# A two-layer graph attention kernel: first loads in another order, first projection spread over ten slots, one unit's copies on VectorE

## The chip, the cores and the metric

The kernel runs on 1 core of one Trainium2 chip. The metric is device time in microseconds (us) from the start to the end of an execution. The engines are TensorE (PE; its weight loads are shown as PEld), VectorE (DVE), ScalarE (ACT), GpSimd (POOL) and SyncE (SP). SP issues every transfer of this kernel, and 16 DMA engines carry it out.

## What is computed

x is 128 graphs of 128 nodes with 384 numbers each, adj is 128 matrices of 128x128. Each of two layers adds a 12-headed attention over a normalised x; the two layers differ in where adj enters and in the projection at the end.

```
h = max(layernorm(x), 0)
q, k, v = h @ W0q + b0q, h @ W0k + b0k, h @ W0v + b0v            # 12 heads of 32
a = softmax(where(adj > 0, q k^T / sqrt(32) + beta * adj, -9e15))
x = x + a v

h = max(layernorm(x), 0)
q, k, v = h @ W1q.T, h @ W1k.T, h @ W1v.T + b1v
a = q k^T / sqrt(384) + adj        # a row of zeros alone gives zeros
x = x + (softmax(a) v) @ W1o.T + b1o
```

## The kernel before

Four graphs (512 tokens) make a group, a group in one layer makes a unit: 64 units. The program is a row of phases of 12 slots each, and in a phase several units are in different stages at once: one is normalised (`norm`), one projected (`project`), one attended (`attend`), and the last chunks of the one before are finished (`tail`). A slot is a chunk of attention: 4 heads of one graph, so 3 slots are a graph. Each engine runs its own in-order program, and semaphores tie them together. Where in a slot a step stands is set by hand, by constants such as `SPLIT_AT = (2, 0)` (slots later, place in the slot), and by tables.

*Normalising.* VectorE makes the statistics of a graph (L813 to L825), ScalarE centres it (L717). For the first two units ScalarE also makes the fp16 high half (L726) and VectorE the low half (L835); SP then turns both into h by a DMA transpose (L518), one a graph. GpSimd raises the variance to -0.5 (L568).

*Weights.* Seven weights are loaded (L457, `load_weight`) and split into w_hi (ScalarE, L658) and w_lo (VectorE, L766), in slots given by LOAD_SLOTS, HIGH_SLOTS and LOW_SLOTS. The first three are staged in the buffers that later hold the stacks.

*Projecting.* A unit has ten jobs of nine matmuls (L999, `job_bank`): six for q and k, four for v. PROJ tables say how many of them stand at three places of each slot. ScalarE makes part_hi of a q or k job (L679, L683), VectorE part_lo (L865, L870); VectorE takes v (L879). SP copies each part_hi twice and each part_lo once into "stack" (L483, L487): 18 copies of 128 KB a unit. The first unit's first copy waits for the third w_lo, since a stack lies over its staging. The scores (L1012) of the third chunk need the last of these copies, and the first matmul of a unit's projection needs all four of its transposes.

*Attention.* In slot s PE makes the scores of chunk s+2, VectorE turns those of chunk s+1 into neg and neg_max (L787), ScalarE takes the exponentials of chunk s (L667), PE transposes the probabilities of chunk s-1 into pt_bank (L1022), and they are copied to probs_t (L692, ScalarE). Three chunks on, PE multiplies them with v (L1035, `o_bank`). In layer 1 five small VectorE steps, reciprocal to inv_wide (L844 to L857), PE's transpose (L1058) and ScalarE's copy inv_t (L699) prepare the scaling; o_norm (L893, VectorE), o_hi (L706, ScalarE), o_lo (L644, GpSimd), the output projection (L1068 to L1072) and result_rows (L901, VectorE) follow. GpSimd adds up neg (L599, L605).

*First phases.* Phase 0 normalises unit 0 and converts three weights. Phase 1 projects unit 0 by PROJ_FIRST, normalises unit 1 (x_second, which lies in probs_t) and makes the first two chunks' scores. Phase 2 attends unit 0 and projects unit 1. The last unit has a phase in which its v is projected by PROJ_LAST_V beside its own attention.

Of the kernel before, what the change touches and what calls it, by code (L numbers as in the profile page):

```python
# [15 lines left out]
KC = DIM // P  # L16
# [30 lines left out]
PROJ_FIRST = ((0, 0, 0),) * 4 + ((4, 4, 3),) * 6 + ((4, 4, 4),) * 2  # L47
PROJ_LAST_QK = ((0, 4, 1), (1, 4, 0), (0, 4, 1), (4, 0, 1), (0, 4, 1), (5, 0, 1), (4, 1, 1), (2, 2, 1), (4, 4, 2),
                (2, 0, 0), (0, 0, 0), (0, 0, 0))
PROJ_LAST_V = ((0, 0, 5), (0, 0, 4), (0, 0, 0)) * GROUP  # L50
# [31 lines left out]
NORM_SLOTS_FIRST = (0, 1, 2, 3)  # L82
SHARED_UNITS = 2
LOW_ROWS_AT = (3, 0)

LOAD_SLOTS = ({}, {}, {0: 3, 3: 4, 6: 5, 9: 6}, {})
HIGH_SLOTS = ({2: 0, 3: 1, 5: 2}, {}, {3: 3, 6: 4, 9: 5}, {0: 6})
LOW_SLOTS = ({4: 0, 6: 1, 8: 2}, {}, {4: 3, 7: 4, 10: 5}, {1: 6})
# [41 lines left out]
class Phase:  # L130
# [9 lines left out]

    def counts(self):
        return self.table or PROJ[self.attend.layer]
# [21 lines left out]
def before():  # L164
# [3 lines left out]
        Phase(project=u(0), norm=u(1), look=u(0), bias=0, weights=1, table=PROJ_FIRST, norm_slots=NORM_SLOTS_FIRST),  # L168
# [81 lines left out]
def layer1_unit(group, off):  # L250

    if not isinstance(group, int):
        return group * 2 + (2 * off + 2)
    return next(n for n in range(UNITS) if layer_and_group(n) == (1, group + off))

# [14 lines left out]
def build(nc, x, adj, w0q, b0q, w0k, b0k, w0v, b0v, beta, w1q, w1k, w1v, b1v, w1o, b1o, out):  # L270
    weights = (w0q, w0k, w0v, w1q, w1k, w1v, w1o)
    w_scale = (QK0_SCALE, QK0_SCALE, W_SCALE, W_SCALE, W_SCALE, W_SCALE, W_SCALE)
    with ExitStack() as ctx:
# [176 lines left out]
        def _(sp):  # L450
# [3 lines left out]
            load_first(0)  # L454
            load_first(1)
            def load_weight(m):
                sp.dma_start(staging(m), weights[m].rearrange("(c p) n -> p c n", p=P)).then_inc(weight_in[m], 16)  # L457

            load_weight(0)
            load_first(2)  # L460
            load_first(3)
# [9 lines left out]
            load_weight(2)  # L471
# [18 lines left out]
            def phase(p):  # L490
                for s in range(SLOTS):
# [38 lines left out]
                    if s == 10 and p.norm is not None and p.norm.layer == 0:  # L530
                        g = p.norm.group
                        if isinstance(g, int) and g < 2:

                            if g == 1:
                                sp.wait_ge(centred_ready, GROUP)
                                sp.dma_start(x_norm[:, :, :], x_groups[2]).then_inc(x_norm_in, 16)
                        elif not isinstance(g, int) or g < GROUPS - 1:
                            sp.wait_ge(centred_ready, p.norm.n * GROUP + GROUP)
                            sp.dma_start(x_norm[:, :, :], x_groups[g + 1]).then_inc(x_norm_in, 16)
                    if p.weights == 0 and s == 5:  # L540
                        sp.dma_start(x_second, x_groups[1]).then_inc(x_second_in, 16)
# [3 lines left out]
            phase(before()[0])  # L545
            sp.dma_start(adj0[:, :, :], adj_groups[0]).then_inc(adj0_in, 16)
            phase(before()[1])
            sp.dma_start(x_res[:, :, :], x_groups[0]).then_inc(x_res_in, 16)
# [106 lines left out]
        def _(act):  # L655
# [73 lines left out]
            def phase(p):  # L729
                for s in range(SLOTS):  # L730
                    for place in range(4):
# [3 lines left out]
                        if place == 2 and u is not None:  # L735
                            copy_turned(u, c)
# [22 lines left out]
        def _(dve):  # L759
# [9 lines left out]
            def biased_scores(u, c):  # L769
# [21 lines left out]
                last.then_inc(neg_ready, 1)  # L791

# [119 lines left out]
            def phase(p):  # L912
                bias_slot = SLOTS - 1 if p.attend is not None else 7
                for s in range(SLOTS + 1):
                    for place in range(3):
# [6 lines left out]
                        if place == 1 and u is not None:  # L922
                            biased_scores(u, c)
# [210 lines left out]
```

## Time and profile before

| | us |
|---|---|
| median of 3 runs | 2221.32 |
| lowest, highest | 2221.24, 2221.51 |
| profiled execution | 2218.76 |
| its span, first to last instruction | 2216.9 |

| engine | busy, share of the span |
|---|---|
| PE | 97% |
| ACT | 92% |
| DVE | 82% |
| POOL | 68% |
| PEld | 64% |

All rows below come from the one profiled execution, with times from the start of its span. A share is an average over all stages; the first 50 us and the last 40 us look different from it, and are read in the timeline and in windows. Operations of one engine overlap a little, so the distance from one start to the next is shorter than the length that is shown.

### The profile page before, as it was taken

The page shows a single profiled execution, that of the slowest core. Times are in us where ns is not written, and L with a number is a line of the kernel's source. Part 1 is how long each engine was busy: PE and PEld are TensorE (multiplying, and loading weights), DVE is VectorE, ACT ScalarE, POOL GpSimd, SP SyncE. Part 2 cuts the span into 40 slices and gives each one's busy share as a digit, 9 for nine tenths or more (in the row PEclk, how much of TensorE's full clock was granted, in tenths as well). Part 3 has the DMA queues.
Part 4 walks back from the last instruction along what each step waited for, and adds up shares of the span by engine and source line. Part 5 has one row for each costly group of instructions (what it writes and reads, how often), then busy time and mean ns, then how long its engine had stood idle before and what let it go on. Part 6 is the DMA issues. An engine that isn't in the chain of part 4 may idle for free.

```text
span 2216.9 us, 75650 instructions
## 1 busy us (share of the span) xinstructions
PE 2158.5 (97%) x19968; PEld 1422.1 (64%) x19968; DVE 1821.3 (82%) x10202; ACT 2049.2 (92%) x7824; POOL 1511.6 (68%) x2407
## 2 busy tenths in 40 slices
PE   5999999999999999999999999999999999999997
PEld 2566666666666666666666666666666666666665
DVE  5888888888888888888888888888888888888787
ACT  4999999999999999999999999999999999999987
POOL 1567766767667767667676677676676766776665
PEclk9999999999999999999999999999999999999999
DMA  9886776678678778675795686787767866766752
GB/s 191 168 134 140 130 138 147 130 131 157 126 137 138 137 143 141 132 143 125 134 159 127 136 139 136 145 136 137 143 130 135 154 130 134 146 132 134 133 103 60
DMA packets 461362, 303.38 MB, mean 137 GB/s; under 512 B 228481, under 2 KB 460929, under 8 KB 460929
## 3 DMA queue, kind: packets, MB, share of 16 engines
q1 hardware_dynamic: 460928, 298.45, 71.2%
q8 instruction: 169, 2.77, 0.6%
q14 instruction: 265, 2.16, 0.4%
HBM read 71.83 MB, written 25.17 MB: 44 GB/s over the span
## 4 chain that ended last, share of the span: by engine, by line
PE 84%; DVE 7%; ACT 4%; issue 3%; DMA 1%; SPq 0%; DVEq 0%; POOL 0%; ACTq 0%
PE job_bank L999 46%; PE pt_bank L1022 13%; PE o_bank L1035 8%; PE score_bank L1012 7%; ACT probs L667 3%; PE inv_bank L1058 3%; PE post_bank L1068 2%; PE post_bank L1069 2%; PE post_bank L1072 2%; PE post_bank L1050 2%; DVE neg L787 2%; DVE part_lo L865 1%; DVE inv_wide L857 1%; DMA x_norm<-in_x 1%; DVE off_zero L848 1%
## 5 line engine op out<-in xcount | busy, mean ns | idle before, releaser
L667 ACT ACTIVATE probs<-neg,neg_max 128x128 f32<-128x128 f32 x3072 | 1189.8, 394 | 47.0 <-DVE neg_max L787 47.0
L999 PE MATMUL job_bank<-h,w_hi 128*128 128x512 f16 x2304 | 725.9, 381 | 27.1 <-DMA h<-o_norm 21.6
L667 ACT ACTIVATION_READ_ACCUMULATOR probs<-neg,neg_max 128x1 f32 x3072 | 596.0, 194 | 0.0
L692 ACT ACTIVATE probs_t<-pt_bank 128x512 f32<-128x512 f32 x768 | 450.1, 586 | 32.0 <-PE pt_bank L1022 29.2
L1022 PE MATMUL pt_bank<-ident,probs 128*128 128x128 f32 x3072 | 464.2, 274 | 11.8 <-ACT probs_t L692 11.4
L999 PE MATMUL job_bank<-h,w_lo 128*128 128x512 f16 x1152 | 438.4, 381 | 0.0
L1022 PEld LDWEIGHTS pt_bank<-ident,probs 128*128 128x128 f32 x3072 | 365.9, 141 | 95.9 <-issue 14.0
L599 POOL TENSOR_TENSOR pair_sum<-neg 128x256 f32<-128x256 f32 x384 | 281.0, 732 | 196.0 <-DVE neg_max L787 180.8
L999 PE MATMUL job_bank<-w_hi,h 128*128 128x384 f16 x1536 | 413.9, 326 | 0.6 <-DVE v L879 0.3
L787 DVE CUSTOM_DVE_ANT_0 neg<-score_bank,bias 128x128 f32<-128x128 f32 x1536 | 354.1, 286 | 23.7 <-issue 22.2
L787 DVE CUSTOM_DVE_ANT_0 neg<-score_bank,adj 128x128 f32<-128x128 f32 x1536 | 353.8, 286 | 13.2 <-issue 10.5
L999 PEld LDWEIGHTS job_bank<-h,w_hi 128*128 128x128 f16 x2304 | 222.0, 98 | 217.4 <-issue 35.8
L1012 PEld LDWEIGHTS score_bank<-stack 96*128 96x128 f16 x3072 | 232.4, 97 | 126.5 <-DVE neg_max L787 6.3
L1012 PE MATMUL score_bank<-stack 96*128 96x128 f16 x3072 | 299.2, 219 | 5.3 <-DMA stack<-part_lo 5.3
L787 DVE DVE_READ_ACCUMULATOR2_ANT neg_max<- 128x1 f32 x3072 | 254.3, 83 | 0.6
L999 PE MATMUL job_bank<-w_lo,h 128*128 128x384 f16 x768 | 250.5, 326 | 0.0
L568 POOL TENSOR_TENSOR rstd<-shift_var,minus_half 128x1 f32<-128x1 f32 x256 | 144.8, 566 | 146.9 <-DVE shift_var L825 145.4
L590 POOL TENSOR_TENSOR h_rows<-h_rows 128x384 f16<-128x384 f32 x248 | 226.7, 914 | 20.7
L618 POOL TENSOR_TENSOR x_mid<-x_res,o_rows 128x384 f32<-128x384 f32 x128 | 127.9, 999 | 140.8 <-DVE o_rows L908 97.1
L1035 PE MATMUL o_bank<-probs_t,v 128*32 128x128 f32 x6144 | 220.8, 277 | 0.0
L870 DVE SCALAR_TENSOR_TENSOR part_lo<-job_bank,part_hi 128x512 f16<-128x512 f32 x192 | 132.5, 690 | 105.4 <-ACT part_hi L683 103.4
L605 POOL TENSOR_TENSOR four_sum<-pair_sum 128x128 f32<-128x128 f32 x384 | 176.6, 460 | 32.1
(75 smaller groups left out, 3507.6 us busy)
## 6 DMA issues: line engine op xcount, KB each, us to landing
stack<-part_hi SPq DMA_DIRECT2D x768, 128.0 KB, 3.5
stack<-part_lo SPq DMA_DIRECT2D x384, 128.0 KB, 3.8
x_res<-in_x SPq DMA_DIRECT2D x32, 768.0 KB, 5.8
out_x<-result_rows SPq DMA_DIRECT2D x128, 192.0 KB, 3.4
x_norm<-in_x SPq DMA_DIRECT2D x30, 768.0 KB, 6.2
adj<-in_adj SPq DMA_DIRECT2D x64, 256.0 KB, 3.8
h<-h_rows SPq DMA_TRANSPOSE x252, 3.9
x_norm<-in_x SPq DMA_DIRECT2D x4, 192.0 KB, 4.0
```

The costliest lines, as they stand in the source:

```text
L568: pool.tensor_tensor(rstd[:, b:b + 1], shift_var[:, b, 1:2], minus_half[:, :], ALU.pow).then_inc(rstd_done, 1)
L590: pool.tensor_tensor(h_rows[b % 2][:, 1, :], h_rows32[:, :], h_rows[b % 2][:, 0, :], ALU.subtract).then_inc(h_rows_ready, 1)
L599: pool.tensor_tensor(pair_sum[:, :, :], neg[c % 2][:, :, 0:NODES // 2], neg[c % 2][:, :, NODES // 2:NODES], ALU.add).then_inc(pair_sum_don ...
L605: pool.tensor_tensor(four_sum[b % 2][:, first:first + HC, :], pair_sum[:, :, 0:NODES // 4], pair_sum[:, :, NODES // 4:NODES // 2], ALU.add ...
L667: last = act.activation(probs[c % 2][:, h, :], neg[c % 2][:, h, :], ACT.Exp, bias=neg_max[:, b, first + h:first + h + 1], scale=-1.0, accu ...
L692: act.activation(probs_t[b % 2][:, first:first + HC, :].rearrange("p h q -> p (h q)"), pt_bank[:, :], ACT.Copy).then_inc(probs_t_ready, 1)
L787: last = dve.tensor_tensor_reduce(out=neg[c % 2][:, h, :], in0=score_bank[c % 2][:, P * h:P * (h + 1)], in1=bias, scale=(-1.0 / SCORE0 if ...
L870: last = dve.scalar_tensor_tensor(part_lo[t][:, c, :], job_bank[j % 2][:, :], scale, part_hi[t][:, c, :], ALU.mult, ALU.subtract)
L999: last = pe.matmul(to, stationary, moving, start=(m == 0), stop=(m == MATMULS - 1))
L1012: last = pe.matmul(score_bank[c % 2][:, P * h:P * (h + 1)], q[0:3 * HEAD, c % KC, h, nodes], k[0:3 * HEAD, c % KC, h, nodes], start=True, ...
L1022: last = pe.transpose(pt_bank[:, P * h:P * (h + 1)], probs[c % 2][:, h, :], ident[:, :])
L1035: last = pe.matmul(o_bank[d:d + HEAD, f:f + P], v32[u.parity][:, b, HEAD * h:HEAD * (h + 1)], probs_t[b % 2][:, h, :], start=True, stop=True)
```

## The change

- The four blocks of the first group's x are loaded ahead of all weights. The third weight is loaded in slot 7 of phase 0, behind the four transposes. The conversions of the three weights move to slots 4 to 9.
- x of the second group, adj of the first, x_norm of the third group and x_res are issued between phase 0 and phase 1. The last two stood in and behind phase 1.
- PROJ_FIRST: 9 matmuls in each of the first ten slots, in place of four empty slots and then 11 or 12. The second unit is normalised in slots 2 to 5 in place of 0 to 3, and its transposes stand correspondingly later.
- PROJ_LAST_V: 3 matmuls in each slot. In that phase (`alone`) the scores stand at place 0 of a slot, not at place 4.
- The last unit's 12 copies of pt_bank are VectorE's, at place 2 of the slot.

```diff
-PROJ_FIRST = ((0, 0, 0),) * 4 + ((4, 4, 3),) * 6 + ((4, 4, 4),) * 2
+PROJ_FIRST = ((3, 3, 3),) * 10 + ((0, 0, 0),) * 2
...
-PROJ_LAST_V = ((0, 0, 5), (0, 0, 4), (0, 0, 0)) * GROUP
+PROJ_LAST_V = ((0, 0, 3),) * SLOTS
...
+NORM_SLOTS_SECOND = (2, 3, 4, 5)
...
-LOAD_SLOTS = ({}, {}, {0: 3, 3: 4, 6: 5, 9: 6}, {})
-HIGH_SLOTS = ({2: 0, 3: 1, 5: 2}, {}, {3: 3, 6: 4, 9: 5}, {0: 6})
-LOW_SLOTS = ({4: 0, 6: 1, 8: 2}, {}, {4: 3, 7: 4, 10: 5}, {1: 6})
+LOAD_SLOTS = ({7: 2}, {}, {0: 3, 3: 4, 6: 5, 9: 6}, {})
+HIGH_SLOTS = ({4: 0, 5: 1, 7: 2}, {}, {3: 3, 6: 4, 9: 5}, {0: 6})
+LOW_SLOTS = ({6: 0, 7: 1, 9: 2}, {}, {4: 3, 7: 4, 10: 5}, {1: 6})
...
+        self.alone = begin > 0
...
+def turned_by_vector(u):
+
+    return isinstance(u.n, int) and u.n == UNITS - 1
...
-            load_first(0)
-            load_first(1)
...
+            for b in range(GROUP):
+                load_first(b)
             load_weight(0)
-            load_first(2)
-            load_first(3)
             load_weight(1)
...
             phase(before()[0])
+            sp.dma_start(x_second, x_groups[1]).then_inc(x_second_in, 16)
             sp.dma_start(adj0[:, :, :], adj_groups[0]).then_inc(adj0_in, 16)
+            sp.wait_ge(centred_ready, GROUP)
+            sp.dma_start(x_norm[:, :, :], x_groups[2]).then_inc(x_norm_in, 16)
+            sp.dma_start(x_res[:, :, :], x_groups[0]).then_inc(x_res_in, 16)
             phase(before()[1])
-            sp.dma_start(x_res[:, :, :], x_groups[0]).then_inc(x_res_in, 16)
...
-                        if place == 2 and u is not None:
+                        if place == 2 and u is not None and not turned_by_vector(u):
                             copy_turned(u, c)
...
+            def copy_turned(u, c):
+                dve.wait_ge(probs_turned, chunk(u, c))
+
+                b, first = c // KC, c % KC * HC
+                if first == 0 and some(u.n * GROUP + b - 1):
+                    dve.wait_ge(pv_done, u.n * GROUP + b - 1)
+                dve.tensor_copy(probs_t[b % 2][:, first:first + HC, :].rearrange("p h q -> p (h q)"),
+                                pt_bank[:, :]).then_inc(probs_t_ready, 1)
...
-                        if place == SCORES_AT and u is not None:
+                        if place == (0 if p.alone else SCORES_AT) and u is not None:
```

SP at the end of phase 0, before: the third weight (its destination is called "stack" there) is issued ahead of the transposes of h, and x of the second group (destination probs_t) ahead of the fourth.

```order
L457 DMA stack<-in_L_gnn_Wv 128x3x384
L518 DMA_TRANSPOSE h<-h_rows 128x6x128 [waits h_rows_ready] x2
L518 DMA_TRANSPOSE h<-o_t 128x6x128 [waits h_rows_ready]
L541 DMA probs_t<-in_x 128x4x384
L518 DMA_TRANSPOSE h<-o_norm 128x6x128 [waits h_rows_ready]
L546 DMA adj<-in_adj 128x4x128
L518 DMA_TRANSPOSE h<-h_rows 128x6x128 [waits h_rows_ready] x2
L518 DMA_TRANSPOSE h<-o_t 128x6x128 [waits h_rows_ready]
L483 DMA stack<-part_hi 32x4x512 [waits part_hi_ready,w_lo_ready]
```

The same place of the changed kernel:

```order
L523 DMA_TRANSPOSE h<-h_rows 128x6x128 [waits h_rows_ready] x2
L523 DMA_TRANSPOSE h<-o_t 128x6x128 [waits h_rows_ready]
L523 DMA_TRANSPOSE h<-o_norm 128x6x128 [waits h_rows_ready]
L463 DMA stack<-in_L_gnn_Wv 128x3x384
L545 DMA probs_t<-in_x 128x4x384
L546 DMA adj<-in_adj 128x4x128
L548 DMA x_norm<-in_x 128x4x384 [waits centred_ready]
L549 DMA x_res<-in_x 128x4x384
L488 DMA stack<-part_hi 32x4x512 [waits part_hi_ready,w_lo_ready]
```

Five loads now stand between the fourth transpose and the first stack copy, and the second unit's transposes moved behind stack copies.

VectorE on the last unit, before: the end of a chunk's score work, then o_norm, v, and the next chunk.

```order
L787 ISA neg,neg_max<-score_bank,adj 128x128
L787 ISA neg_max 128x1
L893 TENSOR_TENSOR o_norm<-o_bank,inv_t 128x384 [waits o_lo_ready,inv_t_ready,pv_done]
L879 SCALAR_TENSOR_TENSOR v<-job_bank,bv_rows 128x384 [waits pv_done,job_done]
L762 MEMSET carrier_v 128x1 [waits pair_sum_done,exp_done,scores_done]
```

The same place, changed:

```order
L789 ISA neg,neg_max<-score_bank,adj 128x128
L789 ISA neg_max 128x1
L801 COPY probs_t<-pt_bank 128x512 [waits probs_turned]
L904 TENSOR_TENSOR o_norm<-o_bank,inv_t 128x384 [waits o_lo_ready,inv_t_ready,pv_done]
L764 MEMSET carrier_v 128x1 [waits pair_sum_done,exp_done,scores_done]
```

A copy stands between a chunk's score work and o_norm, and v has gone one slot later.

PE on the last unit, before: the transpose of inv_wide, v matmuls, and then the scores.

```order
L1058 MATMUL inv_bank<-ident,inv_wide 128x128 [waits inv_t_ready,inv_wide_ready]
L1058 MATMUL inv_bank<-ident,inv_wide 128x128 x2
L999 MATMUL job_bank0<-w_hi5,h1 128x384 x2
L999 MATMUL job_bank0<-w_lo5,h1 128x384
L999 MATMUL job_bank0<-w_hi5,h1 128x384
L1012 MATMUL score_bank1<-stack11,stack01 128x128 [waits neg_ready]
```

Changed, the same scores:

```order
L1026 MATMUL score_bank1<-stack11,stack01 128x128 [waits neg_ready]
L1026 MATMUL score_bank1<-stack11,stack01 128x128 x3
L1082 MATMUL post_bank<-w_hi6,o_hi 128x384 [waits o_hi_ready,result_ready]
L1083 MATMUL post_bank<-w_lo6,o_hi 128x384
L1082 MATMUL post_bank<-w_hi6,o_hi 128x384
L1083 MATMUL post_bank<-w_lo6,o_hi 128x384
```

They now stand ahead of the output projection, the product with v and the transpose of inv_wide in that slot.

## Rows read from the trace of the kernel before

**Rows 1.** The page: an engine's busy time, share of the span, number of instructions.
```profile
PE 2158.5 (97%) x19968; PEld 1422.1 (64%) x19968; DVE 1821.3 (82%) x10202; ACT 2049.2 (92%) x7824; POOL 1511.6 (68%) x2407
```

**Rows 2.** Timeline, 0 to 22 us: start, length, engine, line, operation, [idle before <-released by].
```profile
7.66 0.56 DVE L813 BATCH_NORM_STATS2 stats<-x_norm 128x6 f32<-128x384 f32 x1 [2.50 <-DMA x_norm<-in_x]
...
8.86 4.33 SPq L518 DMA_TRANSPOSE h<-h_rows  x2
...
12.83 0.61 DVE L835 SCALAR_TENSOR_TENSOR o_norm<-inv_wide,rstd,o_norm 128x384 f16<-128x384 f32 x1 [0.56 <-DVE o_t L835]
...
14.98 1.16 ACT L658 ACTIVATE w_hi<-stack 128x1152 f16<-128x1152 f32 x1 [2.19 <-DMA stack<-in_L_gnn_Wv]
...
15.88 1.22 SPq L518 DMA_TRANSPOSE h<-o_norm  x1
...
16.17 1.36 DVE L766 SCALAR_TENSOR_TENSOR w_lo<-stack,w_hi 128x1152 f16<-128x1152 f32 x1 [1.46 <-ACT w_hi L658]
...
21.58 1.01 PE L999 MATMUL job_bank<-h,w_hi 128*128 128x512 f16 x2 [21.58 <-DMA h<-o_norm]
```

**Rows 3.** DMA issues, 0 to 22 and 23 to 27.5 us: KB each, us to landing.
```profile
probs_t<-in_x SPq DMA_DIRECT2D x1, 768.0 KB, 5.5
...
h<-o_t SPq DMA_TRANSPOSE x1, 2.8
```

**Rows 4.** Windows, all engines: us, busy (count) PE PEld DVE ACT POOL, PEclk, DMA, GB/s.
```profile
36.00:47.00 11.00, 7.76 (x50) 4.29 (x48) 5.15 (x24) 3.98 (x17) 0.00 (x0) 1.00 1.17 130
...
48.00:54.00 6.00, 4.75 (x21) 3.19 (x22) 2.70 (x24) 1.53 (x5) 0.73 (x3) 0.50 1.08 354
```

**Rows 5.** Timeline, 40 to 52 us.
```profile
40.53 0.60 SPq L487 DMA_DIRECT2D stack<-part_lo  x1
...
49.25 0.61 PE L1012 MATMUL score_bank<-stack 96*128 96x128 f16 x4 [5.30 <-DMA stack<-part_lo]
...
51.20 0.56 DVE L813 BATCH_NORM_STATS2 stats<-x_norm 128x6 f32<-128x384 f32 x1 [6.46 <-DMA x_norm<-in_x]
...
51.68 0.29 DVE L787 CUSTOM_DVE_ANT_0 neg<-score_bank,bias 128x128 f32<-128x128 f32 x1
```

**Rows 6.** The stack copies of part_hi (L483), 0 to 60 us: issue lengths, and landing.
```profile
L483 SPq DMA_DIRECT2D stack<-part_hi x14: 573/602/700, 28.1 to 56.4; - x14
...
DMA to landing us min/median/max: 2.9/4.3/7.8
```

**Rows 7.** Windows of three graphs of the last unit, columns as in rows 4.
```profile
2177.33:2185.34 8.01, 6.87 (x75) 5.05 (x74) 5.97 (x38) 7.45 (x33) 5.32 (x8) 1.00 0.09 28
...
2185.34:2192.86 7.52, 6.38 (x71) 4.71 (x70) 6.76 (x38) 6.96 (x31) 5.65 (x9) 1.00 0.08 27
...
2192.86:2200.38 7.52, 6.38 (x71) 4.71 (x70) 6.44 (x38) 6.95 (x31) 6.70 (x10) 1.00 0.08 29
```

**Rows 8.** Timeline, 2171 to 2211 us.
```profile
2171.34 0.69 DVE L870 SCALAR_TENSOR_TENSOR part_lo<-job_bank,part_hi 128x512 f16<-128x512 f32 x1 [1.25 <-ACT part_hi L683]
...
2171.95 0.22 DVE L844 RECIPROCAL inv<-total 128x12 f32<-128x12 f32 x1
...
2173.59 0.28 DVE L787 CUSTOM_DVE_ANT_0 neg<-score_bank,adj 128x128 f32<-128x128 f32 x1
...
2182.70 0.29 DVE L787 CUSTOM_DVE_ANT_0 neg<-score_bank,adj 128x128 f32<-128x128 f32 x1 [1.80 <-POOL pair_sum L599]
...
2185.69 0.73 POOL L599 TENSOR_TENSOR pair_sum<-neg 128x256 f32<-128x256 f32 x1
...
2185.89 0.56 DVE L848 TENSOR_SCALAR off_zero<-neg_max 128x12 f32<-128x12 f32 x1
...
2188.32 0.28 DVE L787 CUSTOM_DVE_ANT_0 neg<-score_bank,adj 128x128 f32<-128x128 f32 x1
...
2210.43 0.49 ACT L699 ACTIVATE inv_t<-inv_bank 128x384 f32<-128x384 f32 x1 [2.14 <-PE inv_bank L1058]
```

**Rows 9.** VectorE's copies out of PSUM (L886): min/median/max ns, first and last start.
```profile
L886 DVE COPY o_t<-o_bank x128: 546/557/559, 62.4 to 2113.9; 128x384 f32<-128x384 f32 x128
```

More of the change, by code:

```diff
@@ L167, in before @@
         Phase(norm=u(0), weights=0, norm_slots=NORM_SLOTS_FIRST),
-        Phase(project=u(0), norm=u(1), look=u(0), bias=0, weights=1, table=PROJ_FIRST, norm_slots=NORM_SLOTS_FIRST),
+        Phase(project=u(0), norm=u(1), look=u(0), bias=0, weights=1, table=PROJ_FIRST, norm_slots=NORM_SLOTS_SECOND),
         Phase(attend=u(0), project=u(1), norm=u(2), look=u(1), bias=1, weights=2),
@@ L470, in _ @@
             sp.dma_start(bo_rows[:, :], b1o.partition_broadcast(P)).then_inc(consts_in, 16)
-            load_weight(2)
             def stack(u, j):
@@ L531, in phase @@
                         g = p.norm.group
[L532 to L537, printed above, removed]
+                        if not isinstance(g, int) or 2 <= g < GROUPS - 1:
                             sp.wait_ge(centred_ready, p.norm.n * GROUP + GROUP)
                             sp.dma_start(x_norm[:, :, :], x_groups[g + 1]).then_inc(x_norm_in, 16)
-                    if p.weights == 0 and s == 5:
-                        sp.dma_start(x_second, x_groups[1]).then_inc(x_second_in, 16)
                     if p.weights is not None and s in LOAD_SLOTS[p.weights]:
@@ L923, in phase @@
                             biased_scores(u, c)
+                        u, c = unit_of_chunk(p, s - 1)
+                        if place == 2 and u is not None and turned_by_vector(u):
+                            copy_turned(u, c)
                         u, b = finished(p, s, place, O_T_AT)
```

## The prediction

> **What bounds the kernel now.** The totals come first: PE is busy 97% of a 2216.9 us span [rows 1]. The slices show that its clock and its business are flat from the second slice to the last but one, so the steady part can't be touched by this change, which edits the first 50 us and the last 35 us. What an edit there is worth is the shift it gives to everything behind it. The profiled execution took 2218.76 us, 1.9 more than its span, and 2.6 less than the median of the runs, 2221.32. I make the sum against the profiled one and carry the difference over. The measurement tells about 0.2%, 4.4 us, from no change.
>
> *The start*, read in the timeline. VectorE idles 2.50 us at 7.66 for the third block of x, which was issued behind the first weight; the low half of the fourth block of h ends at 13.44; its DMA transpose is issued at 15.88, behind the 768 KB of the next x, and takes until 21.58, 5.7 us, when PE starts [rows 2]. Then comes the part that is easily missed. The score operands are built by 18 copies of 128 KB ("stack") from 28.1 on [rows 6]. They are issued every 0.65 us, the last at 40.53, but the DMA engines are full from 36 to 47 us at 130 GB/s, which is 1.01 us for a copy [rows 4, 5]. Their time from issue to landing grows from 2.9 us [rows 6] to 8.7, until PE gets the third chunk's operands at 49.25, after 5.30 us of idling, and VectorE, which waits 6.46 us for the next x_norm, gives its third chunk only at 51.68 [rows 5]. Behind that stand ScalarE's exponentials and the whole rest. So the end of the start is set by the DMA engines, not by PE.
>
> *The end*. On the last unit a graph takes 7.52 us; ScalarE is busy 6.96 of them, VectorE 6.76 and 6.44, PE 6.38 [rows 7]. ScalarE is the nearest to a bound, but VectorE follows at once.
>
> **The start, step by step.** All four blocks of x now come ahead of the weights. The 2.50 us wait goes, and the two conversions of 1.36 us stand behind the fourth block [rows 2]; ScalarE's own row of four centre and four high operations keeps a part of that, so I put the last low half at 10.4, not 13.44 (estimate). SP reaches its first transpose when it has issued the constants, at 7.1. Two transposes took 4.33 us to issue, one 1.22 [rows 2]; so the fourth is issued at about 12.8. It lands in 2.8 us when the queue is empty [rows 3], in 5.7 behind the large load [rows 2]; 3.1, near the empty case: PE starts at 15.9 instead of 21.58.
>
> That gain of 5.7 us is not carried on. The third weight is now issued behind the transposes, at 14.1. 768 KB alone took 5.5 us [rows 3], 576 KB some 5.0, so it lands at 19.1. Its two conversions take 1.16 and 1.36 us [rows 2], the bias columns 0.4, and ScalarE's first part_hi waits for these; with 0.7 for itself it ends at 22.8, and the first stack copy goes out then: 5.3 us ahead of 28.1 [rows 6]. PE finishes its first two jobs and waits 1 to 2 us for it. SP waits there as well (stack waits for the third w_lo), and behind it stand only stack copies and the second unit's transposes.
>
> The DMA engines have more in front of them, though: the third weight, x of the second group, adjacency, x_norm and x_res, 3.2 MB, where the last two (1.5 MB) used to come behind the stack copies. At 354 GB/s [rows 4] that is 9.0 us from 16 on: 25. The first stack copy then lands at about 26.3 instead of 31.0. Between 31.0 and 49.25 seventeen further copies and one transpose landed [rows 5, 6]: 17 x 1.01 leaves 1.0 for the transpose. In the change all four transposes of the second unit's h stand behind the fourth copy group or later, the last two behind all copies, and PE's first matmul of the next phase waits for the last: 26.3 + 17.2 + 4.0 = 47.5. It runs two matmuls at the lower clock (0.50 of full speed, 1.2 GHz, is granted there after the idling [rows 4]; PE will have idled from about 39, so again) and the scores, 1.4 us in all: VectorE's third chunk starts at 48.9 instead of 51.68, because its x_norm is long in. **Start: -2.8 us.** If the transposes are issued in 1.22 us each and the loads follow sooner, it is -4.6; if the loads run at the rate of their mixed windows and the first copy lands at 28.5, -0.8.
>
> The Trainium skill, "DMA: Bandwidth & Descriptors", section "Queues, rings and completion order", says that each DMA engine takes a ring's descriptors in order. That speaks against moving two large loads ahead of small urgent copies; by it the 1.5 MB cost the copies their full 4.3 us, as in my sum, and if the engines shared instead, the first copies would land about 2 us sooner.
>
> Norms of the second unit one slot or two later, and PE's even distribution over ten slots, cost nothing: both lie beside the full DMA engines.
>
> **The end, step by step.** Twelve copies of 128x512 go from ScalarE to VectorE. A VectorE operation of the same size out of PSUM lasts 0.69 us and the next starts 0.61 after it [rows 8]: three are 1.83 us for a graph. VectorE's 6.60 (mean of the two windows) become 8.43, more than the 7.52 of a graph now. So VectorE becomes the bound of the last unit. The bounds of its 6.60: the five small steps that make inv_wide run from 2171.95 to 2173.59, 1.64 us; on the last unit they run from 2185.34, where the second window begins, to 2188.32, 2.98 us, and off_zero in them took 0.56 and ended with GpSimd's pair_sum, issued first [rows 8]. GpSimd is busy 5.65 to 6.70 of 7.52 us [rows 7], and in the change its sums still fall beside them; I take 2.6. Without waits a graph would be 7.45, with all of them 8.8. Copies out of PSUM are not stretched: 128 of them took 546 to 559 ns [rows 9].
>
> The Trainium skill, "SBUF — State Buffer", section "SBUF: two separate sides", calls this an exclusive lock of a port pair, held for a whole instruction, that VectorE takes with two SBUF inputs or in a two-port mode. By it the stretch belongs to the small steps alone, as the rows have it, and the period lies in my bounds.
>
> Graph by graph: the first window (8.01 us) has 1.80 us of idle VectorE for scores that PE issued late [rows 7, 8]. Scores at place 0 take that away; but the inverse still waits for PE's transpose behind the output projection, and ScalarE for VectorE's o_norm, which is now behind a copy: 8.6, +0.6. Two full graphs: 2 x 0.91 = +1.8. From the tenth slot's inverse on, ScalarE has no copies left, the last exponentials start 0.5 sooner, and PE's last transposes don't wait for two ScalarE copies in a row: inv_t, at 2210.43 now [rows 8], comes 1.2 us sooner relative to that inverse. **End: +1.2 us** (-1.6 without waits for GpSimd, +3 with all).
>
> **Sum.** 2218.76 - 2.8 + 1.2 = 2217.2 for the profiled execution, 2219.7 for the median.
>
> **Rivals**, each in terms of the median. (a) *VectorE isn't held by GpSimd in the new order*: a period of 7.45, end -1.6, sum -4.4: 2216.9. For it speaks 1.64 us at 2171.95; against it the 2.98 us of the graph at 2185.34. 0.13. (b) *The DMA engines aren't the bound of the start*: the 5.3 us of the first stack copy come through: -4.1, 2217.2. The full window at 130 GB/s speaks against it. 0.10. (c) *The gain of the start is nil*: PE starts early, but the second h's transposes, now last, land at 49 or later: only the +1.2 of the end stays, 2222.5. It needs a first copy at 29; 0.12. (d) *Slower*: VectorE's copies put PE's transposes, which need the bank, into a round trip with it: exponentials, transpose 0.6, copy 0.6, and each small step stretched, so that a graph takes over 9.3 us. Four graphs at +2, less 1.2, less the start: +4, 2225.3. A bank is free only when VectorE has come round to it, which speaks for it; that the copy stands right behind 0.86 us of score work, longer than the transpose needs, against it. 0.05.
>
> **Numbers.** The forecast has 0.60, with its own range 2217.5 to 2221.5. The range down to 2216.0 takes in (a) and (b), up to 2223.0 takes in (c). Faster by over 0.2%: only where a good start and a good end meet, 0.18. Slower by over 0.2%: (d), 0.05. Within: 0.77.
>
> **What would show it.** PE's first matmul at 15.9 and first stack copy issued near 22.8; DMA engines full until 47; PE idle from 39 to 47; VectorE's third chunk at 48.9. On the last unit VectorE busy over 95%, ScalarE idle over 1.5 us a graph, a period of 8.4. I'm wrong if the period is under 7.7 or the third chunk stands before 46.5 or after 51.

## The result, and the profile after

| | before | after |
|---|---|---|
| median of 8 runs, us | 2221.22 | 2214.74 |
| lowest, highest | 2217.97, 2223.24 | 2211.43, 2217.28 |
| profiled execution, its span | 2218.76, 2216.9 | 2216.25, 2214.4 |

The ratio is 0.9972, 95% interval 0.9961 to 0.9983: 6.2 us faster (3.8 to 8.7). The forecast was 2219.7 with a range from 2216.0 on, so the kernel is faster than the whole range, 2216.0 to 2223.0. The profiled execution of before lies 2.5 us under its median, that of the change 1.5 us above; why is read below under *The middle*.

*The start.* Timeline of the changed kernel, 7 to 48 us (start, length, engine, line, operation, [idle before <-released by]); lines have moved: L488, L492 are the stack copies, L523 the transposes of h, L1013 the jobs, L789 the score work.

```profile
16.03 1.01 PE L1013 MATMUL job_bank<-h,w_hi 128*128 128x512 f16 x2 [16.03 <-DMA h<-o_norm]
...
22.31 1.33 SPq L488 DMA_DIRECT2D stack<-part_hi  x2
...
30.23 1.25 SPq L523 DMA_TRANSPOSE h<-h_rows  x1
...
42.89 1.01 PE L1013 MATMUL job_bank<-h,w_hi 128*128 128x512 f16 x2 [4.14 <-DMA h<-o_t]
...
44.38 0.28 DVE L789 CUSTOM_DVE_ANT_0 neg<-score_bank,bias 128x128 f32<-128x128 f32 x1 [3.31 <-issue]
...
47.02 0.06 DVE L764 MEMSET carrier_v<- 128x1 f32 x1 [1.29 <-PE score_bank L1026]
```

PE starts at 16.03 and the first copy is issued at 22.31, both as forecast. But PE gets the last of the four transposed blocks at 42.89, not at 47.5, and the third chunk stands at 44.38, 7.3 us ahead of 51.68 [rows 5]. Why shows in the landing times of the copies of part_hi (L488, up to 40 us) and in the windows (us, busy (count) PE PEld DVE ACT POOL, PEclk, DMA, GB/s). The last window is one of the kernel before, just ahead of that of [rows 4]:

```profile
DMA to landing us min/median/max: 3.4/4.0/4.6
```

```profile
27.00:32.00 5.00, 4.71 (x24) 2.10 (x23) 4.05 (x16) 4.45 (x8) 1.09 (x2) 1.00 1.14 231
34.00:37.00 3.00, 2.49 (x17) 1.30 (x15) 2.20 (x8) 0.00 (x0) 0.00 (x0) 1.00 1.25 134
```

```profile
29.00:36.00 7.00, 7.00 (x33) 3.14 (x33) 4.20 (x8) 2.31 (x4) 0.00 (x0) 1.00 1.04 164
```

The first twelve copies, issued ahead of the first transpose, moved at 231 GB/s in this window, 0.57 us each. From the first landing (22.31 + 4.3 = 26.6) to the twelfth (29.5 + 3.6 = 33.1) it is 0.59 us each, less than the 0.65 us in which SP issues them: the time to landing shrinks and no backlog builds up. The six copies behind them share the queue with transposes, at 134 GB/s, and the landing grows to 5.3 us. Before, two stretches have to be told apart. The first six copies landed from 31.2 to 35.5, 0.86 us each (the window at 164 GB/s holds transposes too). Behind them the fourth transpose was issued, at 32.15, and from then on it is the 130 GB/s of [rows 4]; the last twelve copies landed from 37.5 to 49.2, 1.06 us each.

Part of the 7.3 us goes at once. PE comes out of 4.14 us of idling at half clock, and VectorE waits 1.29 us for the fourth chunk's scores: it stands at 47.05 against 53.06, 6.0 us earlier. Before, PE came back at half clock as well, at 49.25, but it was ahead of VectorE, which waited for x_norm until 51.20 [rows 5]. As the landmark for the start I use from here on the sixth copy o_t<-o_bank: 104.40 before, 98.19 after, **-6.2 us**.

*The middle.* The shift of the copies o_t<-o_bank is still -6.0 us at 994.21 (1000.20 before) and -3.0 at 1041.54 (1044.53 before). In between lies a seam of the program where PE stops for some 3 us. PE's timeline and a window of the changed kernel:

```profile
1026.23 0.61 PE L1013 MATMUL job_bank<-h,w_hi 128*128 128x512 f16 x1 [3.13 <-issue]
```

```profile
1024.00:1036.00 12.00, 9.77 (x68) 6.28 (x69) 6.13 (x40) 6.96 (x28) 2.53 (x5) 0.72 0.05 14
```

PE stood still for 3.13 us (before: 2.67) and then ran until 1032 at half clock, which it didn't in the profiled execution of before, where the granted clock of this window is 1.00. That is scatter of single executions, some 3 us, and not the change. The run end_only below has the start of before, stood still for 2.65 us at the seam, and ran at half clock there too (granted 0.68 from 1030 to 1035). The medians show the whole 6 us, the two profiled executions only 2.5. Similar stretches at half clock stand near 2174 and 2206 us in some of the traces below. For that reason the landmarks, and not the ends of the spans, are compared here.

*The end.* Windows of the three graphs that answer to [rows 7]:

```profile
2174.37:2182.68 8.31, 8.06 (x84) 5.64 (x83) 7.78 (x40) 7.26 (x34) 6.01 (x9) 1.00 0.08 27
2182.68:2190.76 8.08, 6.98 (x71) 4.51 (x70) 7.84 (x39) 5.63 (x27) 5.69 (x9) 1.00 0.07 25
2190.76:2198.49 7.73, 7.04 (x70) 4.53 (x69) 7.49 (x40) 5.63 (x27) 6.71 (x10) 1.00 0.08 29
```

In the two full graphs (the last two lines) VectorE is busy 97% and is the bound, as forecast; ScalarE has 2.1 to 2.5 us to spare. From the second inverse (2174.37) to the last result the unit takes 37.06 us, before 36.60: **+0.46 us**.

### The profile page after: what moved, and what is told of

It is laid out like the page before. It is cut to its first block, busy times and chain, and to the rows that moved or that the text cites. A ratio compares the mean times of both kernels' runs of the same rounds, so it can differ in the third digit from the quotient of the medians.

```text
span 2214.4 us, 75651 instructions
## 1 busy us (share of the span) xinstructions
PE 2163.4 (98%) x19968; PEld 1422.9 (64%) x19968; DVE 1825.4 (82%) x10214; ACT 2043.8 (92%) x7812; POOL 1510.6 (68%) x2407
## 4 chain that ended last, share of the span: by engine, by line
PE 83%; DVE 8%; ACT 4%; issue 3%; SPq 1%; DMA 1%; DVEq 0%; POOL 0%; ACTq 0%; POOLq 0%
PE job_bank L1013 45%; PE pt_bank L1036 13%; PE o_bank L1049 7%; PE score_bank L1026 7%; PE inv_bank L1072 3%; ACT probs L669 3%; PE post_bank L1082 2%; PE post_bank L1086 2%; PE post_bank L1083 2%; PE post_bank L1064 2%; DVE neg L789 2%; DVE part_lo L876 1%; DVE inv_wide L868 1%; DVE live L863 1%; DVE row_sum L857 1%
## 5 line engine op out<-in xcount | busy, mean ns | idle before, releaser
L1013 PE MATMUL job_bank<-h,w_hi 128*128 128x512 f16 x2304 | 726.6, 381 | 26.1 <-DMA h<-o_norm 16.0
L694 ACT ACTIVATE probs_t<-pt_bank 128x512 f32<-128x512 f32 x756 | 443.0, 586 | 31.5 <-PE pt_bank L1036 28.7
L1013 PE MATMUL job_bank<-h,w_lo 128*128 128x512 f16 x1152 | 438.5, 381 | 0.0
L1013 PE MATMUL job_bank<-w_hi,h 128*128 128x384 f16 x1536 | 415.2, 326 | 1.2 <-DVE v L890 0.8
L789 DVE CUSTOM_DVE_ANT_0 neg<-score_bank,bias 128x128 f32<-128x128 f32 x1536 | 354.0, 286 | 29.1 <-issue 27.5
L789 DVE CUSTOM_DVE_ANT_0 neg<-score_bank,adj 128x128 f32<-128x128 f32 x1536 | 353.8, 286 | 10.1 <-issue 9.1
L1013 PEld LDWEIGHTS job_bank<-h,w_hi 128*128 128x128 f16 x2304 | 222.0, 98 | 216.3 <-issue 30.1
L789 DVE DVE_READ_ACCUMULATOR2_ANT neg_max<- 128x1 f32 x3072 | 254.2, 83 | 0.6
L1013 PE MATMUL job_bank<-w_lo,h 128*128 128x384 f16 x768 | 250.5, 326 | 0.0
```

What stands on the lines that cost most here:

```text
L694: act.activation(probs_t[b % 2][:, first:first + HC, :].rearrange("p h q -> p (h q)"), pt_bank[:, :], ACT.Copy).then_inc(probs_t_ready, 1)
L789: last = dve.tensor_tensor_reduce(out=neg[c % 2][:, h, :], in0=score_bank[c % 2][:, P * h:P * (h + 1)], in1=bias, scale=(-1.0 / SCORE0 if ...
L1013: last = pe.matmul(to, stationary, moving, start=(m == 0), stop=(m == MATMULS - 1))
```

## The experiments

"Landmark" is the sixth o_t copy, relative to the 104.40 of before; "unit" is the last unit from its second inverse to its last inv_t (L699 or L701), 33.10 us before and 33.56 after. Both come from one profiled execution of each kernel. Ratios are to the kernel before, with a 95% interval.

| run | third chunk at | landmark | unit | ratio |
|---|---|---|---|---|
| after | 44.38 | -6.2 | 33.56 | 0.9972 (0.9961 to 0.9983) |
| start_only | 45.53 | -6.0 | | 0.9976 (0.9966 to 0.9986) |
| end_only | 51.66 | -0.1 | 33.57 | 1.0004 (0.9995 to 1.0013) |
| loads_behind | 47.81 | -3.7 | 33.56 | 0.9985 (0.9975 to 0.9994) |
| loads_ahead | 51.20 | +0.3 | | 0.9997 (0.9988 to 1.0006) |
| loads_right_ahead | 52.31 | +1.9 | 33.10 | 1.0016 (1.0006 to 1.0026) |
| norm_early | 47.05 | -4.2 | | 0.9978 (0.9968 to 0.9988) |
| proj_packed | 51.07 | -0.1 | 33.55 | 0.9999 (0.9989 to 1.0009) |
| later1_act | 43.83 | -7.5 | 31.83 | 0.9952 (0.9938 to 0.9966) |
| later2_split | 43.37 | -8.4 | 31.75 | 0.9956 (0.9942 to 0.9969) |
| later2_act | 42.52 | -8.6 | 31.81 | 0.9955 (0.9942 to 0.9969) |

Where "unit" is empty, a stretch at half clock lies in it. The third chunk scatters more than the landmark: start_only has the same start as the changed kernel, and 45.53 and 44.38 come together again at -6.0 and -6.2.

**The two halves of the change.** start_only has PROJ_LAST_V, the place of the scores and ScalarE's copies as before; end_only is the kernel before with these three changed.

> The changed kernel with its last unit as before (PROJ_LAST_V, place of the scores, ScalarE's copies): the start of the change alone. The forecast's sum has -2.8 us for it. The trace of the changed kernel has its later start at -6.1 us from 84 us on, so by it: third chunk of VectorE at 44.4, the steady part 6.1 us earlier, and the median 6 us under that of the kernel before (2215.2). If the last unit's edits had brought part of the 6.5 us, the start alone would show under 5 us.

> The kernel before with the last unit of the change (v spread over all slots, scores at place 0, twelve copies on VectorE): the end alone. The forecast has +1.2 us for it; the trace of the changed kernel shows the stretch from the first inverse of the last unit to the last result 0.46 us longer. So: +0.5 us by the trace, +1.2 by the forecast, and periods of 8.3, 8.1 and 7.7 us for the three graphs. If the two parts depend on each other (they are 2100 us apart) it would be another number; I expect none.

Start -6.0 at the landmark, end +0.47 (33.57 against 33.10) and no more than +2.9 us by the interval of end_only. At the landmarks they add up to the change; by the medians they are -5.3 and +0.9 against -6.2, which agrees within the intervals. The gain is the start's alone.

**Which loads stand ahead of the copies.** loads_behind:

```diff
+                        if isinstance(g, int) and g == 1:
+                            sp.wait_ge(centred_ready, GROUP)
+                            sp.dma_start(x_norm[:, :, :], x_groups[2]).then_inc(x_norm_in, 16)
...
-            sp.wait_ge(centred_ready, GROUP)
-            sp.dma_start(x_norm[:, :, :], x_groups[2]).then_inc(x_norm_in, 16)
-            sp.dma_start(x_res[:, :, :], x_groups[0]).then_inc(x_res_in, 16)
             phase(before()[1])
+            sp.dma_start(x_res[:, :, :], x_groups[0]).then_inc(x_res_in, 16)
```

> The changed kernel with x_norm loaded in slot 10 of phase 1 and x_res behind phase 1, as in the kernel before; the stack copies then stand behind 1.7 MB less of loads. Theory A (backlog): copies into bands of 32 partitions are slow, 1.01 us each at 130 GB/s, when the 16 DMA engines reach each of them together, and fast when they come behind a long queue, in which the engines drift apart and work at different copies. Then the copies here run near 130 GB/s from 26 us on, the last transposes land at 45 to 47, and VectorE's third chunk comes at 47 to 50 instead of 44.4: taking 1.5 MB from ahead of them makes them later. Theory B (the rate has nothing to do with the loads; it comes from the order of copies and transposes): the copies run at 180 to 230 GB/s as in the changed kernel, start to land 3 us sooner and are done by 39; the third chunk then waits for x_norm or comes at 42 to 44.

With 1.5 MB less ahead of them the copies are slower: timeline and a window of this run,

```profile
45.23 1.01 PE L1014 MATMUL job_bank<-h,w_hi 128*128 128x512 f16 x2 [6.18 <-DMA h<-o_t]
...
47.32 0.56 DVE L825 BATCH_NORM_STATS2 stats<-x_norm 128x6 f32<-128x384 f32 x1 [6.42 <-DMA x_norm<-in_x]
```

```profile
26.00:34.00 8.00, 7.72 (x39) 3.50 (x38) 6.50 (x24) 7.03 (x12) 1.65 (x3) 1.00 1.16 146
```

PE gets its operands at 45.23 instead of 42.89, and VectorE's x_norm comes later still: it is this wait that sets the third chunk here, at 47.81. The place of the two loads is worth 2.5 us of the 6.2, by both waits together. Theory B falls, since it had 180 to 230 GB/s here. But this run changes two things at once: the loads that are left landed at 22.0, so the queue was empty when the first copy was issued, at 22.63. Which of the two it is, the programs with nothing but copies have to tell.

loads_ahead and loads_right_ahead put the same two loads into the kernel before, once between the phases, once directly ahead of the first stack copy.

> The kernel before with x_norm and x_res issued between phase 0 and phase 1, and nothing else. Theory A (backlog): 1.5 MB stand ahead of the copies, yet these run at 200 GB/s or more once they come (from 32 us on), and the last one lands at 43 to 45 instead of 48: third chunk at 45 to 47 instead of 51.7, the median 4 to 6 us less. Theory B (copies cost 1.01 us each whatever stands ahead): the first copy lands at 32 to 35 and the last at 50 to 52: third chunk at 51 to 53, no gain.

> The kernel before with x_norm and x_res (1.5 MB) issued immediately ahead of the first stack copy, and nothing else; the DMA engines then have a queue of several us when the copies come, which they hadn't in the run with these loads between the phases (there the loads had landed at 27, 2 us before the first copy, and the copies ran at 130 GB/s). Theory A (backlog): the loads end at 33 to 34, the copies behind them run at 200 GB/s or more at first and the last lands at 44 to 47; PE gets the third chunk's operands 2 to 5 us earlier than at 49.25. Theory B (1.01 us a copy, whatever stands ahead): the last copy lands at 51 to 53, the third chunk comes at 52 to 54, the median is 0 to 2 us more than before.

Neither gains, and this took me a step further. In the first the loads had landed by 27.9 us, 1.2 us before the first copy was issued at 29.09, and three transposes stood between: no run of copies behind loads at all. In the second:

```profile
34.00:37.00 3.00, 3.00 (x17) 1.56 (x16) 1.09 (x2) 1.37 (x2) 0.00 (x0) 1.00 1.15 223
39.00:50.00 11.00, 4.17 (x30) 2.23 (x27) 3.97 (x22) 3.29 (x16) 0.00 (x0) 0.88 1.16 132
```

Theory A's fast copies are there, at 223 GB/s, but only six of them: behind these the fourth transpose was issued, at 32.89, and from 39 on it is 132 GB/s for the other twelve. My expectation missed since it took the fast rate to hold to the end. The suspicion: a transpose ends it.

**The other two parts of the start.** norm_early has NORM_SLOTS_SECOND = (0, 1, 2, 3), proj_packed the old PROJ_FIRST.

> The changed kernel with the second unit normalised in slots 0 to 3, not 2 to 5: its four transposes then stand behind copy groups 2, 3, 4 and 5, and a copy group is the last. The prediction put PE's wait for the next phase to the last transpose, behind all copies. Bytes in the queue are the same, so the end of all of them is the same, 42.9, and the third chunk comes within 1 us of 44.4, at 43.5 to 45. If the order mattered (a transpose among copies brings the engines back together), copies of the later groups run at 130 GB/s and the third chunk comes at 45 to 47.

> The changed kernel with the first projection's table as before (four empty slots, then 11 or 12 matmuls): the loads and norms of the change stay. PE has nothing but waits and the same matmuls in the same order in this phase, so I expect its first matmul at 16, the first copy issued at 22.3 and the third chunk within 1 us of 44.4; but ScalarE's and VectorE's steps stand differently between slots: if the parts of the jobs then come behind the norms of the second unit, the first copy goes out 1 to 3 us later and the third chunk at 46 to 48.

In norm_early the first transpose stands behind six copies, not twelve, and a group of copies comes last (PE waits for it until 46.39). Its windows:

```profile
26.00:29.00 3.00, 3.00 (x14) 1.20 (x13) 2.50 (x14) 2.50 (x5) 0.55 (x1) 1.00 1.29 221
31.00:34.00 3.00, 2.81 (x16) 1.34 (x15) 2.34 (x5) 0.69 (x1) 0.00 (x0) 1.00 1.25 122
```

221 GB/s up to the transpose and 122 behind it: 2.0 us lost at the landmark. In proj_packed a transpose is issued at 25.63, ahead of all copies, and the first copy goes out only at 26.96, since the first projection's parts come behind the second unit's norms. By then the loads had landed, at 26.8:

```profile
29.00:34.00 5.00, 5.00 (x21) 2.07 (x19) 2.10 (x6) 2.49 (x4) 0.55 (x1) 0.84 1.18 129
```

No copy is fast, and nothing is left of the gain. How much of the loss is the first copy going out 4.65 us later, and how much the slower copies, no run separates. I had expected the first copy at most 3 us later and the third chunk at 48 at the latest, with no change as the likelier case: a miss.

**The copies by themselves.** Two programs with nothing but copies of the same form, in sections, each executed once.

```python
sp.dma_start(stack[HEAD * r:HEAD * (r + 1), k, :, :], part[:, k // 6, :]).then_inc(landed[k], 16)
```

> The disputed cost by itself: a program that computes nothing of the reference and only moves data, in eleven sections that are separated by waits. Each has 18 copies of 128 KB (128 partitions x 512 fp16) as the stack copies are. Without or with two 768 KB loads issued ahead; with destinations of 32 partitions in turn (bands 0, 2, 1, 0, 1, 2, as in the kernel), all in band 0, or over 128 partitions; once with transposes among them, once issued from two queues. Theory A (each copy is held up by its one band of 32 partitions, and a queue ahead lets the engines work at several): without loads ahead 17 to 19 us for the bands in turn (130 GB/s), with loads ahead 9 to 12 us behind them; all in one band 17 to 19 us with or without loads ahead; over 128 partitions limited only by the issue, 0.65 us each, 12 to 13 us. Two queues: two copies at once, 10 to 12 us. Theory B (no dependence on the queue ahead): the same time with and without loads for each kind of destination. Theory C (rate is that of engine to SBUF accesses of the compute engines, which are absent here): all sections fast.

> Data movement alone again, nothing of the reference is computed: ten sections of the same 18 copies into bands of 32 partitions in turn, with something else issued ahead or among them. In the run before this one a copy took 0.89 us on an empty queue, whatever its destination band, and 0.60 to 0.75 behind two 768 KB loads. Theory D (the loads leave the 16 engines at different places of the queue, and only a transpose, or an empty queue, brings them together again): behind one load 0.6 to 0.8 us a copy, behind four loads 0.6; behind twelve copies over 128 partitions, which leave no such differences, 0.85 to 0.9; with a transpose between the loads and the copies 0.85 to 0.9 from the first on; with one behind the sixth or the twelfth copy, 0.6 to 0.75 up to it and 0.85 to 0.9 behind it. Theory E (it is the length of the queue ahead): behind four loads shorter than behind one, behind twelve wide copies like behind loads, and a transpose changes nothing but its own 1 to 2 us.

VectorE marks each landing with a small operation. The mean distance of landings, in us a copy (131,072 bytes):

| ahead of the 18 copies | copies 1 to 6 | 7 to 12 | 13 to 18 |
|---|---|---|---|
| nothing (three sections) | 0.89 | 0.87 to 0.89 | 0.86 |
| nothing, all in band 0 | 0.89 | 0.99 | 0.73 |
| one load of 768 KB | 0.82 | 0.82 | 0.78 |
| two loads (four sections) | 0.61 to 0.79 | 0.60 to 0.79 | 0.51 to 0.60 |
| two loads, all in band 0 | 0.64 | 0.64 | 0.59 |
| four loads | 0.59 | 0.59 | 0.59 |
| twelve copies over 128 partitions | 0.89 | 0.87 | 0.85 |
| a transpose | 0.96 | 0.95 | 0.85 |
| two loads, then a transpose | 1.01 | 0.98 | 0.96 |
| two loads, a transpose behind copy 6 | 0.63 | 1.17 | 0.95 |
| two loads, a transpose behind copy 12 | 0.73 | 0.61 | 1.18 |
| two loads, transposes behind copies 12, 15 and 18 | 0.73 | 0.64 | 1.28 |
| nothing, issued from two queues | 0.89 | 0.87 | 0.75 |
| nothing, copies over 128 partitions | 0.69 | 0.63 | 0.65 |
| two loads, copies over 128 partitions | 0.38 | 0.37 | 0.52 |
| the same, transposes behind copies 12, 15 and 18 | 0.38 | 0.36 | 0.96 |

Numbers above 1.1 contain the time of a transpose itself, 1 to 2 us; behind copy 6 the following ones took 0.97 to 1.05. SP issues a copy every 0.65 us, which is what the copies over 128 partitions with nothing ahead wait for (the mean DMA share is 0.59 there); the last copies of a section can profit from having nothing behind them.

Three windows: copies_alone with nothing ahead and with two loads ahead (columns here: us, busy DVE POOL, PEclk, DMA, GB/s), and copies_behind with two loads and then a transpose ahead:

```profile
24.41:39.33 14.92, 1.00 (x17) 0.00 (x0) 1.00 1.03 133
47.55:57.15 9.60, 0.94 (x16) 0.00 (x0) 1.00 1.05 199
```

```profile
155.50:171.40 15.90, 0.94 (x16) 0.00 (x0) 1.00 1.10 125
```

Theory B falls here too (the loads do make a difference), theory C (both rates are there with idle compute engines), and so does A's reason (one band behaves like three). Two queues bring nothing either: 14.2 us from the first landing to the last, where theory A had 10 to 12 in all. Theory E falls by the twelve wide copies, which are as many bytes as two loads and bring nothing, and by the transposes. D had the order of the rows right, but not all sizes. Behind a single load a copy took 0.82, hardly less than on an empty queue. And behind a transpose it took 0.95 to 1.05, where D had 0.85 to 0.9: a transpose does more than take the loads' gain away, it makes the copies slower than on an empty queue. It doesn't always: in the kernel before, the first six copies were issued right behind three transposes and took 0.86 us. What differs there no run shows. That the loads leave the 16 DMA engines at different places of the queue is an explanation that fits; no row shows it.

**A better start, and a better end.** later1_act and later2_split move the second unit's norm slots to (3, 4, 5, 6) and (4, 5, 6, 7), so that one and none of its transposes stands ahead of the last copy. In later1_act ScalarE keeps the last unit's copies; in later2_split VectorE takes one of three; later2_act joins the later start with ScalarE's copies. All keep PROJ_LAST_V and the scores at place 0.

```diff
-NORM_SLOTS_SECOND = (2, 3, 4, 5)
+NORM_SLOTS_SECOND = (4, 5, 6, 7)
...
-    return isinstance(u.n, int) and u.n == UNITS - 1
+    return isinstance(u.n, int) and u.n == UNITS - 1 and c % KC == 1
```

> The changed kernel with two edits far apart. Start: the second unit normalised in slots 3 to 6, so that its first transpose stands behind 15 copies and three behind all 18. If a transpose ends the fast mode of the copies, the last copy lands 1 to 2 us sooner than in the changed kernel; the last transpose, for which PE waits, then lands at 42 to 43 if it isn't issued later than 38.2, and the sixth o_t copy stands at 97.5 to 98.5 (changed kernel 98.2). If the order makes no difference, 98.2; if VectorE's later norm work comes late, up to 99.5. End: the copies of the last unit stay on ScalarE, but v is spread and the scores stand at place 0: ScalarE is the bound again with 6.96 us a graph, periods 7.5; the wait for late scores (1.80 us in the first graph) goes: the last unit takes 40.5 to 41.5 us from the first inverse to the last result, where before has 41.98 and the changed kernel 42.44. If v in every slot is what delays the chain, it is 42 to 43.

> The changed kernel with two edits far apart. Start: the second unit normalised in slots 4 to 7, all four transposes behind all 18 copies. The copies then run at 200 GB/s or more to the end, but the last transpose depends on VectorE's and ScalarE's norm work in slot 10: issued at 39 to 40.5, landing at 42.5 to 44: the sixth o_t copy at 98 to 99.5, no better than the changed kernel. End: of three copies of a graph one is VectorE's and two are ScalarE's: VectorE 7.2 us a graph and ScalarE 6.4, both under 7.52; without waits a graph takes 7.3 to 7.6 us, and the last unit 41 to 42 us (before 41.98, changed 42.44). If the waits between the engines decide it and not their work, it is 42.5 or more.

> The start of the run with norms in slots 4 to 7 (all four transposes behind all 18 copies) with the end in which ScalarE keeps its copies (v spread, scores at place 0): each was seen once, with another partner. If a transpose is what slows the copies behind it, and not the chance of one execution, the sixth o_t copy stands again within 0.5 us of 96.0, against 98.2 in the changed kernel, and the copies run at 195 GB/s or more until they are done at 36.5. If the start varies by more than that from run to run, it stands between 95 and 98. The last unit from the second inverse to the last result: 35.3 us at the full clock (before 36.60, changed kernel 37.06). Median 2210 to 2212, 9 to 11 us under the kernel before and 3 to 5 under the changed one.

The landing of the part_hi copies of later2_split, the window over all copies, and PE's restart:

```profile
DMA to landing us min/median/max: 4.4/4.5/4.6
```

```profile
26.00:36.00 10.00, 8.43 (x45) 4.00 (x43) 8.32 (x29) 5.53 (x9) 1.64 (x3) 1.00 1.15 202
```

```profile
42.51 0.59 PE L1013 MATMUL job_bank<-h,w_hi 128*128 128x512 f16 x2 [3.34 <-DMA h<-o_t]
```

The copies run at 202 GB/s, the pace at which SP issues them, and the landmark is 2.2 us earlier than in the changed kernel, 2.4 in later2_act. I had expected no gain, since the last transpose is issued later (38.87): it is, but it finds the copies nearly done. The landmark of later1_act lies 0.6 us under the range I had given it and that of later2_split 2.0 us; later2_act came out as expected.

Only a part of this is the queue's. PE gets its operands at 42.97 in later1_act, 42.51 in later2_split and 41.65 in later2_act, against 42.89 in the changed kernel: a gain of -0.1, 0.4 and 1.2 us. The rest goes with PE's clock (read from the rows; no run isolates it). In the changed kernel PE had idled 4.14 us and needs 1.01 us for its first two matmuls; in these three it had idled 3.51, 3.34 and 3.05 us and needs 0.59. In later2_split the granted clock stays at 1.00, and the fourth chunk stands at 44.80 instead of 47.05. In the other two it falls to 0.50 some 1 to 2 us later. So the whole gain of later1_act over the changed kernel at the landmark (1.2 us), and most of that of later2_split, is the restart.

The last unit takes 1.3 us less than before with either division of the copies (31.75 to 31.83 against 33.10), so v in every slot with the scores first gains, and the twelve copies on VectorE cost 1.7 us against this. later2_act (0.9955) took 2209.95 us against 2219.69 of the kernel before in the same session, 9.7 us less. No session has it beside the changed kernel; by the landmark and the unit it should be 4.1 us faster than that (2.4 + 1.75, an estimate).

## Why the prediction was wrong

- *PE's start, first copy issued*: right (15.9 and 22.8 forecast, 16.03 and 22.31 measured).
- *Loads in front of the copies, first copy landed at 26.3*: right. It was issued at 22.31 and landed 4.3 us later, at 26.6, behind x_res, which had landed at 26.2 (25 forecast). The Trainium skill, "DMA: Bandwidth & Descriptors", section "Queues, rings and completion order", has a ring served in order on each DMA engine, and these landings agree. What I made of it was wrong: the 1.5 MB don't cost the start 4.3 us, taking them away made it 2.5 us later.
- *17 further copies at 1.01 us*: **the step that failed**. The eleven copies behind the first took 0.59 us each, not 1.01, and that alone is 4.6 us, the whole way from 47.5 to 42.89. The 1.01 us was read from 36 to 47 us of before, behind a transpose that stood among the copies. I took it for the price of a copy anywhere, though the first six copies of before, at 0.86, already spoke against that; the rows shown left them out. Copies alone behind loads and a transpose show 0.96 to 1.01 again, behind loads without one 0.60 to 0.79. In the change twelve copies stand between the loads and the first transpose. The forecast carried a rate from one order of the queue into another. The rest of the sum held: six copies and four transposes took 9.8 us (33.1 to 42.89), where 1.01 and 1.0 us each give 10.1.
- *Norm slots and the distribution of PE's matmuls cost nothing*: wrong by the same step. They decide how many copies pass before a transpose, and when the first goes out: 2.0 us by norm_early, all of the gain by proj_packed.
- *PE's clock at the restart*: right, 0.50 of full speed. But it also costs at the fourth chunk, which I didn't count: of the 7.3 us 1.3 are gone there.
- *The end, +1.2 us*: mechanism right, VectorE bound at 97%; size +0.46. The five inverse steps took 2.33 and 1.97 us in the two full graphs, where I had put 2.6; 8.08 and 7.73 less these leave 5.75 and 5.76, my 8.43 less 2.6 was 5.83. So most of the miss there is that one term, by 0.27 and 0.63. Why they were shorter than before (2.98 and 2.65) no run shows. The first graph gave +0.30 (0.6 forecast), the tail -0.61 (-1.2 forecast); VectorE's last copies and PE's transposes wait for each other there, 0.35 to 0.51 us a time, but what each wait costs wasn't isolated.
- *Rivals*: (b) came nearest, with 2217.2, and was half right: the first twelve copies land at SP's pace and aren't held up by the DMA engines. Behind the first transpose the landing grows again, to 5.3 us, and these engines decide when PE gets its operands. (a), (c) and (d) didn't occur. My own marks said the start's step is wrong if the third chunk stands before 46.5; it stands at 44.38.

## What to carry to other kernels

A transfer's price depends on what stands ahead of it in its queue. Before carrying a rate of DMA from one place to another, read which kinds of transfer stood in front where it was measured; here the same copy costs 0.6, 0.9 or 1.0 us. When small copies and DMA transposes share a queue, try to let the copies go in one run, behind large loads, and the transposes behind them. The more copies passed before the first transpose, the better, from six to twelve (2.0 us at the landmark); beyond that PE's operands came at most 1.2 us sooner, and a second effect, PE's clock at its restart, brought as much. And two edits in one change can each be needed for the gain: undone alone, the distribution of PE's matmuls took all of it away.

## What the hardware showed

- 18 copies of 128 KB from 128 partitions to 32, mean distance of the first twelve landings: 0.87 to 0.89 us on an empty queue or behind 12 wide copies, 0.82 behind one load of 768 KB from memory, 0.59 to 0.79 behind two or four, 0.95 to 1.01 behind a DMA transpose (copies_alone, copies_behind). The mean busy share of the 16 DMA engines is 0.97 to 1.10 over each of these sections, so the share doesn't tell the fast copies from the slow ones.
- The destination band hardly matters (0.87 us a copy all in one band, 0.88 for three in turn), the number of destination partitions does: 0.37 us for 128 partitions, 0.64 for 32, both behind two loads.
- PE may come back from a wait at half clock or not, in programs that are alike up to there: at the seam near 1030 us at full clock after 2.67 us of idling (before), at half clock after 2.65 us (end_only), and at half clock for 6 us after 3.13 us (the changed kernel). Before and the changed kernel drift 3 us apart by it.
- What stays open: why loads speed up the copies behind them, why a transpose ends that, and why the first six copies of the kernel before weren't slowed to 1.0 us by the transposes ahead of them. No view of the trace separates the 16 engines.
